# Three program blocks made one around a retention layer, and its weight split moved

## The reference

```
x = x + L0_attn(layernorm(x))   # delta-rule memory attention, 16 heads
x = x + L0_ffn(layernorm(x))    # 16 experts, the best 2 of each token, and a shared expert
x = x + L1_attn(layernorm(x))   # retention: Q, K turned by position, scores times a decay, times V
x = x + L1_ffn(layernorm(x))    # 8 experts, the best 1 of each token
```

```
Q = xpos(X @ W_Q); K = xpos(X @ W_K, downscale=True); V = X @ W_V
att = einsum('bnh,bmh->bnm', Q, K) * D[None]     # D[n, m] = gamma ** (n - m) where n >= m
return att @ V
```

## Time and profile before

| | |
|---|---|
| median of 3 runs | 744.07 us (743.4 to 746.38) |
| the profiled execution | 749.53 us |
| its span, first to last instruction | 747.7 us |
| TensorE busy | 654.7 us (88%) |
| VectorE busy | 413.3 us (55%) |
| ScalarE busy | 339.4 us (45%) |
| GpSimd busy | 314.3 us (42%) |
| mean granted clock of TensorE | 0.949 |

### The profile page before, as it was taken

One profiled execution on the slowest core, in us unless ns is written; L12 is line 12 of the kernel. 1 busy time (PEld: TensorE's weight loads), 2 busy tenths in 40 slices (PEclk: granted clock), 3 DMA queues, 4 the chain that ended last, 5 costly groups with the idle time before them and its releaser, 6 DMA issues. The chain is left out here.

```text
span 747.7 us, 12362 instructions
## 1 busy us (share of the span) xinstructions
PE 654.7 (88%) x4144; PEld 544.1 (73%) x4144; DVE 413.3 (55%) x1119; ACT 339.4 (45%) x834; POOL 314.3 (42%) x383
## 2 busy tenths in 40 slices
PE   4889989989989989989999986999999529984897
PEld 3668878979979879879789885875656318873554
DVE  6778495394593692781873727662222178355233
ACT  3666757566566665665665642123333203000210
POOL 4665644353344435425420305146665318110454
PEclk9999999999999999999999998899999859985799
DMA  8010110200100100100100414942233241028440
GB/s 265 20 57 29 30 56 1 64 29 20 46 29 29 35 28 28 35 28 30 35 1 4 110 64 161 411 145 85 93 85 85 98 153 45 1 77 317 131 113 22
DMA packets 31313, 57.89 MB, mean 77 GB/s; under 512 B 4670, under 2 KB 17952, under 8 KB 31264
## 3 DMA queue, kind: packets, MB, share of 16 engines
q1 hardware_dynamic: 24256, 42.03, 16.7%
q0 software_dynamic: 4896, 13.12, 6.1%
q10 hardware_dynamic: 2112, 2.10, 0.8%
HBM read 48.06 MB, written 10.09 MB: 78 GB/s over the span
## 5 line engine op out<-in xcount | busy, mean ns | idle before, releaser
L892 DVE RECIPROCAL denominators<-readings 128x2 f32<-128x2 f32 x128 | 21.2, 165 | 145.4 <-PE readings L567 144.7
L427 POOL TENSOR_TENSOR w_high<-xn,ones 128x256 fp32r<-128x256 f32 x84 | 53.2, 665 | 76.8 <-PE ahead L215 35.5
L567 PEld LDWEIGHTS readings<-memory_copy,sigma 128*128 128x128 f32 x512 | 75.1, 191 | 13.9 <-ACT memory_copy L764 5.0
L567 PE MATMUL readings<-memory_copy,sigma 128*128 128x129 f32 x512 | 78.9, 276 | 4.0 <-ACT memory_copy L764 3.8
L773 ACT ACTIVATE memory_reading<-readings,denominators 64x128 f32<-64x128 f32 x256 | 78.7, 357 | 5.3 <-DVE denominators L892 3.3
L764 ACT ACTIVATE memory_copy<-memory 128x258 f32<-128x258 f32 x128 | 50.2, 392 | 62.0 <-PE memory L577 48.0
L898 DVE SCALAR_TENSOR_TENSOR minus_delta<-readings,denominators,v 64x128 f32<-64x128 f32 x240 | 73.8, 347 | 4.2
L577 PE MATMUL memory<-minus_delta,sigma_k_tokens 128*128 128x129 f32 x480 | 73.2, 275 | 0.0
L1196 POOL DMA_INDIRECT xs_e<-rows_e,gather_at_e x46 | 44.9, 976 | 65.3 <-DVE scatter_at_e L1597 39.7
L1341 PE MATMUL up_e<-weights_e,xT_e 128*128 x184 | 68.8, 498 | 0.8 <-issue 0.8
L749 ACT ACTIVATE x<-ahead 128x512 f32<-128x512 f32 x60 | 35.9, 598 | 72.9 <-PE ahead L215 28.1
(11 more groups left out here) (267 smaller groups left out, 1438.5 us busy)
## 6 DMA issues: line engine op xcount, KB each, us to landing
weights_e<-experts SPq DMA_DIRECT2D x24, 608.0 KB, 11.8
xn<-L_attn_Wq SPq DMA_DIRECT2D x8, 512.0 KB, 3.8
xn<-L_attn_Wk SPq DMA_DIRECT2D x7, 512.0 KB, 3.8
xn<-L_attn_Wv SPq DMA_DIRECT2D x7, 512.0 KB, 3.9
wo<-L_attn_Wo SPq DMA_DIRECT2D x1, 2048.0 KB, 13.9
rows_e<-xn ACTq DMA_DIRECT2D x4, 512.0 KB, 7.9
x<-L_attn_x SPq DMA_DIRECT2D x4, 256.0 KB, 3.5
x<-L_attn_x SPq DMA_DIRECT2D x2, 512.0 KB, 3.6
```

The lines of the kernel that those rows point to most:

```text
L427: last = pool.tensor_tensor(w_high[i][:, :, of], w_stage[:, :, of], one, ALU.mult)
L567: last = pe.matmul(KQ[g][:, hh * MC:(hh + 1) * MC], sqk[:, GROUP * g + hh, pair, 2 * par:2 * par + 2, :], mz[g][:, hh, :], start=True, sto ...
```

## The change

The expert layer e0, retention and the expert layer e1 write their instructions into one block that `build` opens, so that no barrier stands between them, and this block is opened with `no_gpsimd_drain=True`: GpSimd has no drain at its end. The attention keeps its own block ahead. Most of the diff is only the indentation of the bodies, which is left out here.

What the barriers ordered is ordered otherwise:

- SyncE waits for the last read-back (`read_back`, which is e0's `y_loaded[1]`) ahead of the tables, and for `added` (`earlier_done`) ahead of e1's stores and weights.
- Router and table of e1 go to `Carried`, at space that the read-back used, and SyncE loads them in retention, after xn of half 0.
- On GpSimd all five splits of the retention weights stand directly behind e0's last scatter, ahead of both calls of `invert`; the wait for xn of half 1 is gone.

```diff
 class Carried:
+        columns = table_columns(E1, K1)["first"][1]
+        self.next_router = flat[:, 12 * D:12 * D + KD * E1].rearrange("p (k e) -> p k e", k=KD)
+        self.next_table = flat[:, 13 * D:13 * D + columns]
+        self.next_router_loaded, self.next_table_loaded = sem("next_router_loaded"), sem("next_table_loaded")
...
 def sparse_layer(...)
-        consts = sb("consts", [P, table.shape[1]])
+        consts = carried.next_table if out is not None else sb("consts", [P, table.shape[1]])
...
-        router = sb("router", [P, KD, E])
+        router = carried.next_router if out is not None else sb("router", [P, KD, E])
...
-        router_loaded, table_loaded, weights_loaded = sem("router_loaded"), sem("table_loaded"), sem("weights_loaded")
+        if out is None:
+            router_loaded, table_loaded = sem("router_loaded"), sem("table_loaded")
+        else:
+            router_loaded, table_loaded = carried.next_router_loaded, carried.next_table_loaded
+        weights_loaded = sem("weights_loaded")
...
-        with nc.Block() as block:
             @block.sync
             def _(sp):
+            if out is None:
                 sp.dma_start(router[:, :, :], w["router"].rearrange("(k p) e -> p k e", p=P))\
                   .then_inc(router_loaded, 16)
                 sp.dma_start(consts[:, :], table).then_inc(table_loaded, 16)
-                if out is not None:
+            else:
+                sp.wait_ge(earlier_done, 4)
                     for half in range(2):
                         sp.dma_start(rows[half * HALF:(half + 1) * HALF, D:2 * D].rearrange("(t p) d -> p t d", p=P),
                                      x[:, half * TPH:(half + 1) * TPH, :]).then_inc(rows_stored, 16)
...
                 for b in range(NB - BEHIND, NB):
                     scatter(b)
-                if out is None:
-                    norm.invert(pool, N + 1, 0)
...
-    return join_last
+    return join_last, y_loaded[1]
...
 def retention(...)
-        with nc.Block() as block:
             @block.sync
             def _(sp):
+            sp.wait_ge(read_back, 16 * K0)
                 for i, t in enumerate(tables):
                     sp.dma_start(cos_sin[:, i, :], t).then_inc(tables_loaded, 16)
                 sp.dma_start(decay[:, :], decay_in).then_inc(decay_loaded, 16)
+            sp.wait_ge(norm.xn_done, NT * 2 + TPH)
+            sp.dma_start(carried.next_router[:, :, :], next_w["router"].rearrange("(k p) e -> p k e", p=P))\
+              .then_inc(carried.next_router_loaded, 16)
+            sp.dma_start(carried.next_table[:, :], next_w["table"]).then_inc(carried.next_table_loaded, 16)
...
                     pool.wait_ge(high_done, i + 1)
                     pool.tensor_tensor(w_low[i][:, :, :], w_stage[i][:, :, :], fr(w_high[i][:, :, :]),
                                        ALU.subtract).then_inc(w_split, 1)
-                    if i == 0:
-                        pool.wait_ge(w_split, 1)
-                        norm.invert(pool, 2, 1)
-                        pool.wait_ge(norm.xn_done, NT * 2 + NT)
+            for half in range(2):
+                norm.invert(pool, 2, half)
                 for u in range(4):
...
+        return added
...
 def build(nc, ins, out):
-        join_last = sparse_layer(*common, "e0", E0, K0, mixture0, tiles, next_w=(ins["W_Q"], ins["W_K"], ins["L1_attn_W_V"]),
-                     signals=signals)
-        retention(*common, [ins[n] for n in ("cos_q", "sin_q", "cos_k", "sin_k")], ins["decay"], join_last)
-        sparse_layer(*common, "e1", E1, K1, mixture1, out=out)
+        with nc.Block(no_gpsimd_drain=True) as block:
+            join_last, read_back = sparse_layer(
+                block, *common, "e0", E0, K0, mixture0, tiles,
+                next_w=(ins["W_Q"], ins["W_K"], ins["L1_attn_W_V"]), signals=signals)
+            retained = retention(block, *common, [ins[n] for n in ("cos_q", "sin_q", "cos_k", "sin_k")], ins["decay"],
+                                 join_last, read_back, mixture1)
+            sparse_layer(block, *common, "e1", E1, K1, mixture1, out=out, earlier_done=retained)
```

More of the change, by code:

```diff
@@ L1119, in scatters, with _ @@
             return len(range(ring, NB, RING))
[L1121 to L1123 removed]
+        @block.sync
+        def _(sp):
+            if out is None:
                 sp.dma_start(router[:, :, :], w["router"].rearrange("(k p) e -> p k e", p=P))\
@@ new lines, in _ @@
+            else:
+                sp.wait_ge(earlier_done, 4)
+                for half in range(2):
+                    sp.dma_start(rows[half * HALF:(half + 1) * HALF, D:2 * D].rearrange("(t p) d -> p t d", p=P),
+                                 x[:, half * TPH:(half + 1) * TPH, :]).then_inc(rows_stored, 16)
+            if shared:
+                tiles.load(sp, stage[2], 2, stage_loaded)
+            for e in range(E):
+                sp.dma_start(weights[:, e, :], w["experts"][e, :, :]).then_inc(weights_loaded, 16)
@@ new lines, in _ @@
+            if shared:
+                for i in range(3):
+                    sp.dma_start(carried.retention_w[i], next_w[i].rearrange("(k p) n -> p k n", p=P))\
+                      .then_inc(carried.retention_w_loaded[i], 16)
+            for ring in range(RING):
+                sp.wait_ge(scattered[ring], 16 * scatters(ring))
+            if out is None:
+                for half in range(2):
+                    if half:
+                        sp.wait_ge(y_loaded[0], 16 * K)
+                    for k in range(K):
+                        first = k * T + half * HALF
+                        sp.dma_start(y[k][half], results[first:first + HALF, :].rearrange("(t p) d -> p t d", p=P))\
+                          .then_inc(y_loaded[half], 16)
@@ new lines, in _, with high, copy_v @@
+        @block.scalar
+        def _(act):
+            act.wait_ge(w_loaded[0], 16)
+            act.activation(w_high[0][:, :, :], w_stage[0][:, :, :], ACT.Copy).then_inc(high_done, 1)
+            for half in range(2):
+                norm.high(act, 2, half, B[0:4])
+            def high(u):
+                qk, half = units[u]
+                act.wait_ge(turn_done, 2 * u + 2)
+                act.activation(qk_high[qk][:, :, half * HALF:(half + 1) * HALF], turned[u % 2][:, :, :], ACT.Copy)\
+                   .then_inc(qk_high_done, 1)
+            def copy_v(b):
+                act.wait_ge(v_ready, 2 * b + 2)
+                act.activation(v[:, 2 * b:2 * b + 2, :], B[4 + b][:, :].rearrange("p (t d) -> p t d", t=2), ACT.Copy)\
+                   .then_inc(v_copied, 1)
+            high(0)
+            high(1)
+            copy_v(0)
+            copy_v(1)
+            high(2)
+            copy_v(2)
+            copy_v(3)
+            high(3)
```

1319 lines of the change are left out of this document (638 added, 681 removed).

## The result

| | kernel before | changed kernel |
|---|---|---|
| median of the runs | 744.78 us (743.4 to 746.38, 4 runs) | 738.25 us (736.93 to 739.01, 4 runs) |
| ratio, 95% interval | 1 | 0.9906 (0.988 to 0.9931): 7.0 us less, give or take 1.9 |
| profiled execution, its span | 749.53, 747.7 us | 738.62, 736.8 us |
| mean granted clock | 0.949 | 0.956 |

The account below looks back on a forecast made before the run. TensorE was taken to bound the long stages, with the gain in the seams, chiefly GpSimd's drain at the first. 4.2 + 2.35 + 0.9 = 7.45 us off 744.07 gave 736.6 us, range 733.1 to 740.6.

Parts of the forecast that it names:

- The barrier and the drain at the first seam: First expert layer to retention: VectorE's four products and TensorE's transposes start at 607.4 instead of 610.89, 3.5 us won.
- The moved splits: First seam: splits directly behind GpSimd's last scatter leave the products and `turned` unheld; 0.6 + 0.25 - 0.15 us.
- The first term: First seam: without a split beside the four products, the projection waiting for both xl comes 0.6 us earlier.
- The loss of 0.15: Read-back at the first seam: the last split holds the first product 0.3 us, partly taken up by VectorE's 0.16 wait.
- the 0.25 for `turned`: Retention: `turned` no longer waits for the last split; 0.25 us taken, bounded above by VectorE's 0.32 us wait.
- The second seam: Retention to second expert layer: first transposes 1.8 us earlier, second ones 2.35 us earlier, set by VectorE and GpSimd's rstd.
- The end: Program end: without GpSimd's drain the end follows SyncE, about 746.8 instead of 747.56; 0.9 us won.
- The price is put off: Rival, program end: book-keeping of 92 DMAs falls due after the last one, 7.7 us; time 742.6, chance 0.07.
- It falls on the next GpSimd work: Rival, first seam: 5.2 us ahead of the splits pushes them beside the joins, 4 us lost; 740.6, chance 0.07.
- The queue fills: Rival, second expert layer: its DMAs wait on a software queue not emptied, 13.1 us lost; 749.7, chance 0.04.
- The gap at the first seam is not the drain's: Rival: something that stays holds VectorE to 610.9, leaving the first seam worth 0.7 us; 740.1, chance 0.03.
- The clock stays up: Rival: the high clock lasts through the second expert layer's router, 2.5 us more gained; 734.1, chance 0.12.

Follow-up runs that it names:

- e2: Kernel before with its three blocks and barriers kept, GpSimd's drain left out at the end of all three; 741.48 us, ratio 0.9957.
- e4: Changed kernel with GpSimd's splits back in their old order; 740.80 us, ratio 0.9941 to the kernel before.
- g2: Changed kernel, but GpSimd writes the second expert layer's constants only after xn of half 1; 738.91 us, ratio 0.9899 to the kernel before.
- h2: Changed kernel with only the read-back of half 0 in parts, each with its own semaphore; 740.96 us, ratio 0.9901 to the kernel before.
- e3: Changed kernel with GpSimd's drain put back at the end of its one block; 744.85 us, ratio 0.9993 to the kernel before.
- g3: Changed kernel, but GpSimd's five splits wait until half 0 of the read-back has landed; 743.78 us, ratio 0.9976 to the kernel before.
- e1: As a run, not the layer: kernel before with only GpSimd's drain at the end of the first expert layer left out; 745.71 us, ratio 1.0001.
- g1: Changed kernel measured and profiled once more, nothing altered; 739.80 us, ratio 0.9912 to the kernel before.

## Why the prediction was right, and where it was off

**The barrier and the drain at the first seam** (forecast 3.5). Right. e2 gives 3.0 for the drain, and 0.48 of idle time stays with the barrier: 3.5.

**The moved splits** (forecast 0.6 + 0.25 - 0.15 = 0.7). The first term is right: from the transposes to the first projection it is 3.35 us instead of 3.95, and the projection came 4.17 us earlier, as 3.5 + 0.6 said. The loss of 0.15 wasn't there, because the last split lay beside the first product for 0.12 us only.

From e2 to the changed kernel the first stretch falls by 1.7 us, or 1.2 without the barrier's 0.48.

The term that was mis-sized is the 0.25 for `turned`. From the projection to the last output 0.56 us was won (50.53 to 49.97), and 0.53 of it stands at the start of `turned`: 9.13 us behind the projection in the kernel before, directly behind the last split, and 8.60 in the changed kernel, where it waits for the products. But 0.35 of this is the clock's. It rose 4.9 us behind the first projection's start in the profile before and 4.1 in the one after, so that the transposes of half 1 and all behind them came 0.35 earlier (4.77 against 5.12). The other 0.18 is the order of the splits, close to the 0.25. That VectorE's wait of 0.32 us bounds the term from above is true only for an execution with that clock. With the old order `turned` starts 9.1 us behind the projection, whether the clock rises at 4.9 (before), 3.5 (e2) or 3.1 us (e4). With the splits moved it follows the products, and starts at 8.25 where the clock rose at 3.4 (g2). Between e4 and g2 the move is worth 0.84 us behind the projection, three times the forecast.

The step "TensorE's waits for w_low go too, but only become its slack" is borne out. The wait of 0.78 us at 621.89 is gone, and the wait for q_low at the start of the scores grew from 0.39 to 1.25 us.

**The second seam** (forecast 2.35, measured 1.83). The 1.8 for the idle time was right (2.41 to 0.66), and the transposes ran at the high clock as said (1.07). Two terms behind them were wrong, and of them only one counted. The logits took 1.92, not 3.56 us; that gave nothing, because the second transposes then waited 2.22 us for xn. In h2 the logits took 3.16 us, and the second stretch was 6.70 all the same. The one that counted is xn of half 1. It was to come 0.5 us earlier, by VectorE's 0.55 of idle time at the block end, but it ends 6.65 us behind the last output, 6.64 before. Of the 0.55, 0.26 stays as VectorE's wait for its own addition, and 0.29 goes to GpSimd's constants, which the early table lets run beside xn. g2 takes these 0.29 off again.

The reason given for the transposes' high clock, the earlier start, is not shown: e2 had the high clock with the late start. All nine traces without the barrier have it, and of the three with the barrier one, so an earlier start may make it likelier. An estimate from these rows puts its worth at 0.3 us: with transposes of 1.94 us and logits of 3.56 TensorE would have been done at 666.4, and the second transposes started at 666.08.

**The end** (forecast 0.9). Right: 0.96.

**The rivals.** *The price is put off:* no. The changed kernel ends 0.4 us behind SyncE's branch, the time outside the span is the same 1.8 us, and e3 shows the 7.6 us where a drain stands. *It falls on the next GpSimd work:* no. The first split waits only for ScalarE (1.03 us), and g3 shows what it would have cost there (3.9 us). *The queue fills:* no. The third stretch did not grow, and e1's scatters take 0.98 to 1.02 us. *The gap at the first seam is not the drain's:* it was (runs e1 and e2). The Trainium skill (PSUM — Partial Sum Buffer, "Engine vs sequencer instructions") says that a drain waits until the engine is fully idle. Here GpSimd's drain lasted 2.6, 5.2 and 7.6 us beyond the engine's last work, by the software DMAs since the last drain. Page and trace differ, and the trace decides. *The clock stays up:* it did through the first logits, and fell ahead of the second transposes. That was worth nothing, as xn set the pace, where the rival had priced both logits and the second transposes at 2.5 us.

**The total.** The profile shows 7.5 us, and 7.45 were forecast. That this agrees so closely is luck: the first seam's 0.5 too little and the second's 0.5 too much cancel, and 0.35 of the first is the clock's rise in this pair of executions. The change by itself is worth about 7.2 us by the profile. The ratios say 7.0 us here and 6.6 beside g1 (medians: 6.5 and 6.7). The time came out 1.65 us above the forecast; 0.7 of it is the kernel before, whose median was 744.78 in this set, and the rest lies within the interval.

## What to carry to other kernels

A block end is priced by what its slowest engine has to put in order, and on GpSimd that is every software DMA since its last drain; leaving one drain out only moves the bill to the next, so leaving out only some wins little. Before a wait is called lost time or slack, follow it to the next point that both traces share: here TensorE's 0.78 us came back as a longer wait at the scores, and what counted was GpSimd's own order. A bound read from one trace holds for that trace's clock. When a wait goes, price the work that now starts early by what it lies beside: each elementwise step of 128x512 on GpSimd cost VectorE 0.7 to 1.0 us wherever it met two-input work.

## What the runs showed of the hardware

- GpSimd's drain: 0.085 us for each of 30 software DMAs, 0.084 of 62, 0.082 of 92; 0.05 us beyond its last work where there were none (rows 3 and 4). In e1_first_drain_out the price of e0's 62 was paid 70 us behind the last of them.
- A GpSimd tensor step of 128x512 beside VectorE's products of 128x256 in float32 held them 0.7 us (h2), 0.9 (g3) or 1.0 (e4) for each step. Small constants beside xn, which has one large input, held it 0.3 us in all (1.67 against 1.38, g2).
- The granted clock rose between 2.9 and 6.1 us behind the first projection's start in the twelve profiles. With the splits moved, the time from that start to retention's last output was 49.58 us with a rise at 2.9 (g3), 49.97 with 4.1 (changed kernel) and 50.87 with 6.1 (h2): 1.3 us from one execution to another by the clock alone.
- With TensorE idle the clock fell 2.2 us behind its last output in one execution (before) and 2.8 in another (e1_first_drain_out). In a third it was still up when the transposes came 2.5 us behind the output, and fell 4.2 us behind it (e2_three_blocks_no_drain).
